# Row-max tiles of a causal attention: diagonal tiles taken out of PSUM by ScalarE and masked by GpSimd, own part buffers, and ScalarE's units unrolled

## The chip, the cores and the metric

One core of a Trainium2 chip runs the whole layer in one launch. The metric is the device time of the execution in microseconds (us), as the median of several runs. Engines are named as in the profile: PE is TensorE (matmuls; PEld its weight loads), DVE is VectorE, ACT is ScalarE, POOL is GpSimd and SP is SyncE, which issues most DMAs.

## What is computed

```python
x = L0_attn_x                                  # 2 x 1024 x 256, f32
q, k, v = x @ Wq, x @ Wk, x @ Wv               # 16 heads, 4 KV heads, head size 16
att = q k^T / 4 + alibi + causal mask          # softmax over keys, y = att v
x = layernorm(x + y @ Wo)
# FFN: shared expert silu(x Wg) * (x Wu) @ Wd, and one of 8 routed experts
x = layernorm(x + shared + routed)
```

The change touches the attention alone, and in it mostly the row maximum that the softmax subtracts.

## The kernel before

**Units.** A batch element with one KV head and its 4 query heads is a unit; there are 8 (`NU`). A query block or a key block has 128 rows, 8 of each. Q and K of a unit lie in SBUF as bf16 parts, so that one matmul with 127 contraction rows gives an accurate score. Three buffers of Q and K (`Q6`, `K6`, `STEP` = 3) take turns.

**Two score passes.** The first pass finds each query row's maximum. `max_tile` (PE) makes the scores with queries on the partitions (L529) in one PSUM bank of 512 columns: up to 512 keys of one head, or several heads side by side where the rows are short. Where the key range reaches the diagonal, a second matmul adds a 128x128 mask of -3e38 above it (L531, identity times `mask_qk`). DVE then reduces the bank to one maximum per row and head (`reduce_tile`, L895). These are 39 tiles a unit, listed by `row_max_tiles`, in 3 banks that PE gets back from DVE in order (`s_amax`). Behind the last tile DVE splits the maxima in three bf16 parts with five small operations that wait for each other (`split_max`, L929 to L939). PE transposes the parts (L520), DVE copies them to `mrow` (L946), and SP sends them by DMA to three rows of Q (`max_rows`, L324). This transpose is the 40th entry of the unit's stream and stands behind the first two tiles (`LEAD`) of the next unit.

The second pass makes the scores again, keys on the partitions, with the maximum already subtracted by those rows (`score`, L543, 36 a unit, 3 banks). ACT takes the exponential into SBUF (L820). POOL sets the upper triangle of a diagonal tile to zero (`mask_probs`, L1156). PE multiplies with V in f32 (`weigh`, L554, below W). ACT copies the two result banks out (L829, L834), and SP stores them.

**Order.** PE runs in one hand-written order. A unit has 9 groups, each a string over S (one second-pass score), M (one row-max entry) and W (the `weigh` of the group before): `SHORT` is `SMSMSMWMS`, `LONG` is `SMSMSMWMSM`. The strings alternate and hold 40 M. The Ms of unit u's groups are the later ones of unit u+1 and then the first 14 of unit u+2 (`AHEAD`), so that row maxima are ahead of their use. Unit 0's 39 and the first 14 of unit 1 run in the prologue. ACT's units 0 to 5 are the body of a hardware loop: two turns of three units (`act.Fori`), with units 6 and 7 behind it as plain code. SP has a loop of the same kind.

**Prologue.** Twelve jobs (`JOBS`) project Q, K and V (L499). Each is split in three bf16 parts by ACT, DVE and POOL (L801, L906, L813 or L914, L1128). The first four go to Q and K of units 0 and 1 directly. Jobs 4 to 11 put their parts in one of three buffers (`parts0`, `NP` = 3), and SP stores them in DRAM (L428), from where later units load them (L305, L311). From the fourth of them on, ACT waits until the buffer's store has landed (`s_pw`). SP issues those stores behind 20 DMAs of the direct path (L376, L384), in program order. Between the jobs PE and DVE do the row maxima of unit 0 in lots (`first_tiles`).

## Time and profile before

| what | value |
|---|---|
| median of 3 runs | 568.68 us (566.39, 571.71, 568.68) |
| profiled execution, its own time | 574.12 us |
| its span, first to last instruction | 572.4 us |
| mean granted TensorE clock | 0.957 |
| DMA packets | 39465, 54.97 MB |

The span is what the trace covers; the 1.7 us beside it lie before the first and behind the last instruction. The profiled execution took 5.4 us more than the median. The attention's units lie between 64 and 290 us of the span, the prologue before and the FFN behind them.

### The profile page before, as it was taken

The numbers are of one execution on the slowest core, as the hardware profiler recorded it, in microseconds if no ns is written. First come the engines' busy times: TensorE is split into PE (matmuls) and PEld (weight loads), VectorE is DVE, ScalarE is ACT, GpSimd is POOL, SyncE is SP. The second block draws the span as 40 slices with busy tenths as digits, with TensorE's granted clock in tenths as the row PEclk, the third lists the DMA queues.
The fourth block names the chain that finished last, engine by engine and source line by source line (L and its number), as shares of the span: only waits on it lengthen the run. The fifth ranks groups of instructions, "written<-read, shape, count | busy, mean of one in ns | idle before, by whom it ended". The sixth has DMA issues, their size and how long they took to land.

```text
span 572.4 us, 7851 instructions
## 1 busy us (share of the span) xinstructions
PE 521.7 (91%) x2538; PEld 259.4 (45%) x2538; DVE 299.7 (52%) x624; ACT 231.4 (40%) x465; POOL 172.3 (30%) x240
## 2 busy tenths in 40 slices
PE   5868899999799999998987899989999999999991
PEld 2433333333233333331245754655666565656661
DVE  1759888888678888882045734212212233333332
ACT  3523376767476767677820121001012222232320
POOL 4413111413031313121201106860003545454543
PEclk9979899999989999999977889998999999999997
DMA  7759501927152727210224600221112222222220
GB/s 219 144 146 313 130 23 49 251 75 207 50 135 78 177 82 181 77 38 21 73 81 149 205 0 1 92 93 38 55 52 60 69 61 74 65 74 65 59 53 27
DMA packets 39465, 54.97 MB, mean 96 GB/s; under 512 B 5887, under 2 KB 27971, under 8 KB 39316
## 3 DMA queue, kind: packets, MB, share of 16 engines
q1 hardware_dynamic: 29792, 30.96, 20.7%
q0 software_dynamic: 5952, 19.56, 11.0%
q10 hardware_dynamic: 3680, 3.94, 2.1%
q8 instruction: 21, 0.34, 0.3%
q14 instruction: 20, 0.16, 0.1%
HBM read 34.76 MB, written 17.52 MB: 91 GB/s over the span
## 4 chain that ended last, share of the span: by engine, by line
PE 80%; DVE 6%; ACT 4%; SPq 3%; issue 2%; DMA 1%; another core or an unknown queue 1%; POOL 1%; POOLq 0%; ACTq 0%; DVEq 0%
PE ps L734 14%; PE ps L554 12%; PE ps L529 11%; PE ps L654 10%; PE ps L543 9%; PE ps L753 7%; PE ps L665 5%; DVE mx L895 4%; PE ps L626 3%; PE ps L499 2%; PE ps L531 2%; PE ps L745 2%; ACT probs L820 2%; PE ps L643 1%; SPq L376 1%
## 5 line engine op out<-in xcount | busy, mean ns | idle before, releaser
L895 DVE TENSOR_REDUCE mx<-ps 128x1 f32<-128x512 f32 (+4 forms) x312 | 184.1, 643 | 39.2 <-PE ps L531 22.8
L820 ACT ACTIVATE probs<-ps 128x512 f32<-128x512 f32 x288 | 153.0, 605 | 74.8 <-PE ps L543 70.1
L529 PE MATMUL ps<-qk_or_dn 127*128 127x512 bf16 (+3 forms) x384 | 119.8, 339 | 4.6 <-DVE mx L895 3.5
L543 PE MATMUL ps<-qk_or_dn 127*128 127x512 bf16 x288 | 101.4, 382 | 6.2 <-ACT probs L820 5.7
L1156 POOL TENSOR_SCALAR_AFFINE_SELECT probs<-probs 128x512 f32<-128x512 f32 x64 | 40.6, 634 | 177.8 <-ACT probs L820 177.8
L734 PE MATMUL ps<-wgu,tmp 128*128 x184 | 82.9, 593 | 0.1
L554 PE MATMUL ps<-probs,Vs 128*32 128x512 f32 x576 | 77.1, 608 | 0.7 <-ACT probs L820 0.7
L529 PEld LDWEIGHTS ps<-qk_or_dn 127*128 127x128 bf16 x384 | 37.8, 99 | 78.7 <-DVE mx L895 65.0
L531 PE MATMUL ps<-cb 128*128 128x128 bf16 x256 | 51.8, 227 | 0.0
L1200 POOL DMA_INDIRECT rows<-acc,tok x23 | 22.5, 979 | 91.5 <-DMA acc<-x_all 46.7
L1084 DVE TENSOR_TENSOR tmp<-tmp,ps 128x512 f32<-128x512 f32 x23 | 15.8, 688 | 65.1 <-PE ps L734 65.1
L734 PEld LDWEIGHTS ps<-wgu,tmp 128*128 128x128 f32 x184 | 33.3, 190 | 33.3 <-issue 33.3
L543 PEld LDWEIGHTS ps<-qk_or_dn 127*128 127x128 bf16 x288 | 27.0, 98 | 43.6 <-ACT probs L820 27.2
L753 PE MATMUL ps<-qk_or_dn,tmp 128*128 x184 | 43.6, 380 | 0.8 <-ACT tmp L876 0.8
L876 ACT ACTIVATE tmp<-ps 128x512 f32<-128x512 f32 x23 | 13.7, 597 | 74.9 <-PE ps L745 74.9
L753 PEld LDWEIGHTS ps<-qk_or_dn,tmp 128*128 128x128 f32 x184 | 34.9, 190 | 15.1 <-issue 11.5
L853 ACT ACTIVATE tmp<-ps 128x512 f32<-128x512 f32 x16 | 9.4, 597 | 66.7 <-PE ps L654 61.0
L531 PEld LDWEIGHTS ps<-cb 128*128 128x128 bf16 x256 | 25.7, 100 | 14.9 <-issue 1.6
L665 PE MATMUL ps<-wsd,tmp 128*128 128x256 f32 x128 | 29.7, 391 | 2.4 <-DVE x_all L1072 2.4
L499 PE MATMUL ps<-probs,yU 128*128 128x512 f32 x48 | 26.3, 686 | 6.1 <-DMA yU<-in_wq 6.1
L654 PE MATMUL ps<-probs,wsg 128*128 128x512 f32 x64 | 31.4, 615 | 0.0
L654 PE MATMUL ps<-probs,wsu 128*128 128x512 f32 x64 | 31.3, 612 | 0.0
(117 smaller groups left out, 467.7 us busy)
## 6 DMA issues: line engine op xcount, KB each, us to landing
wgu<-in_gu POOLq DMA_DIRECT2D x8, 1024.0 KB, 6.4
qk_or_dn<-qparts SPq DMA_DIRECT2D x36, 128.0 KB
yT<-yU SPq DMA_DIRECT2D x16, 256.0 KB, 2.4
qk_or_dn<-in_dn SPq DMA_DIRECT2D x8, 512.0 KB, 8.0
tmp<-xs SPq DMA_DIRECT2D x23, 128.5 KB
qparts<-tmp SPq DMA_DIRECT2D x6, 384.0 KB, 4.3
tmp<-yT SPq DMA_DIRECT2D x34, 64.0 KB
xs<-rows POOLq DMA_DIRECT2D x1, 2056.0 KB, 12.8
```

The lines of the kernel that those rows point to most:

```text
L499: mm = pe.matmul(ps[:, 4 + n % 4, :], w, xTc[:, c, kc, :], start=kc == 0, stop=kc == KC - 1)
L529: mm = pe.matmul(o, q, K6[k][0:KROWS, k0:k0 + w], start=True, stop=not masked)
L531: mm = pe.matmul(o[:, diag:diag + P], id16, mask_qk, start=False, stop=True)
L543: pe.matmul(o, K6[k][0:KROWS, kb * P:(kb + 1) * P], Q6[k][0:KROWS, :, qi * P:(qi + 1) * P], start=True, stop=True).then_inc(s_st, 1)
L554: mm = pe.matmul(ps[32 * j:32 * j + VP, 2 + bank, :], Vs[:, u % STEP, kb, :], probs[:, 4 * (s % 3) + p, :], start=begins, stop=ends, skip_ ...
L654: mm = pe.matmul(ps[:, bank + 2 * (n % 2), :], w[:, kc, f * P:(f + 1) * P], x1T[:, kc, c * CH:(c + 1) * CH], start=kc == 0, stop=kc == KC - 1)
L665: mm = pe.matmul(ps[:, 4 + n % 2, 0:H], hidden_part(c, f)[:, t * P:(t + 1) * P], wsd[:, f, :], start=f == 0, stop=f == FC - 1)
L734: mm = pe.matmul(ps[:, 2 * k + half_i, :], xsT[k][:, kc, :], wgu[:, bass.ds(e * (KC * 2 * I) + (kc * 2 * I + half_i * I), I)], start=kc == ...
L753: mm = pe.matmul(ps[:, 7, 0:H], ehT[j % 2][:, f, :], wdn[:, bass.ds(experts[j] * (FC * H) + f * H, H)], start=f == 0, stop=f == FC - 1)
L820: act.activation(probs[:, 4 * (s % 3) + p, :], ps[:, 4 + (4 * s + p) % SB, :], ACT.Exp, scale=SCALE).then_inc(s_exp, 1)
L895: dve.tensor_reduce(o, ps[:, a_bank(u, t), 0:nh * w].rearrange("p (h w) -> p h w", h=nh), AX.X, ALU.max).then_inc(s_amax, 1)
L1156: pool.affine_select(tile, tile, [[0, HG], [1, P]], ALU.is_ge, zero, base=0, channel_multiplier=-1).then_inc(s_mask, 1)
```

## The change

1. **Diagonal tiles apart.** `row_max_tiles` now lists, for each of the 8 query blocks, one DIAG tile (its 128x128 diagonal block for all 4 heads, one full bank), and the keys left of it as LEFT and RIGHT tiles. This makes 38 tiles, 8 of them DIAG. The mask matmul is gone. ACT copies a DIAG bank to one of two SBUF buffers (`copy_diag`, into `dg`), which frees the bank for PE (`s_dcopy`). POOL writes -3e38 above the diagonal (`cut_diag`). DVE reduces it from SBUF four entries later than its place in PE's order (`reduce_order`, `BEHIND`).
2. **Split spread out.** `split_max` becomes two joins behind the last tile of a unit (`join_max`) and four parts, one ahead of each of the next four tiles. The transpose stands behind six tiles of the next unit (`LEAD` = 6).
3. **Order strings.** 39 M a unit. Nineteen of unit u+2 run in unit u (`AHEAD`), 13 of unit 1 in the prologue, and unit 0 takes `LONG` nine times (45 M).
4. **ACT unrolled.** The copies stand in ACT's order as in PE's, and all eight units are plain code.
5. **Own part buffers.** Jobs 4 to 11 each have a buffer, in the region of `wgu`; ACT's wait for `s_pw` is gone. The direct DMAs of unit 0 now all come ahead of those of unit 1.
6. **POOL.** Its gate and up weight loads and `zero_slots` come one group later.

```diff
-LEAD, AHEAD = 2, 14
+LEAD, AHEAD, FIRST_AHEAD = 6, 19, 13
+BEHIND, ND = 4, 2
+SPLITS = 4
-ORDER = (SHORT, LONG) * 4 + (SHORT,)
+ORDER = (SHORT, LONG) * 4 + ("SMSMSMWS",)
...
+def unit_order(u):
+    return (LONG,) * GROUPS if u == 0 else ORDER
...
 def max_tile(u, k, t):
-                    pe.wait_ge(s_amax, i - 2)
+                    beside, diag = freed(i - 3)
+                    if FREED_BY_ACT[i - 3]:
+                        pe.wait_ge(s_dcopy, diag)
+                    else:
+                        pe.wait_ge(s_amax, beside)
...
-                    if masked:
-                        mm = pe.matmul(o[:, diag:diag + P], id16, mask_qk, start=False, stop=True)
...
+            def copy_diag(u, t, bank):
+                n = NQ * u + A_TILES[t][0]
+                act.wait_ge(s_aps, max_index(u, t) + 1)
+                if n >= ND:
+                    act.wait_ge(s_dmax, n - (ND - 1))
+                act.activation(dg[A_TILES[t][0] % ND], ps[:, bank, :], ACT.Copy).then_inc(s_dcopy, 1)
...
-                    if n >= DIRECT + NP:
-                        act.wait_ge(s_pw[n % NP], 16 * ((n - DIRECT) // NP))
-                    act.activation(parts0[n % NP][0:m, 0, :], ps[0:m, 4 + n % 4, :], ACT.Copy).then_inc(s_ph, 1)
+                    act.activation(parts0[n][0:m, 0, :], ps[0:m, 4 + n % 4, :], ACT.Copy).then_inc(s_ph, 1)
...
-            with act.Fori(0, LOOPS, 1) as it:
-                for k in range(STEP):
-                    step(it * STEP + k)
-            for u in range(LOOPS * STEP, NU):
-                step(u, last=u == NU - 1)
+            for u in range(NU):
+                step(u)
...
 def reduce_tile(u, t):
+                if kind == DIAG:
+                    dve.wait_ge(s_dcut, NQ * u + qi + 1)
+                    dve.tensor_reduce(mxd[:, :, qi], dg[qi % ND].rearrange("p (h w) -> p h w", h=HG), AX.X, ALU.max
+                                      ).then_inc(s_dmax, 1)
+                    return
...
+            def cut_diag(u, t):
+                n = NQ * u + A_TILES[t][0]
+                pool.wait_ge(s_dcopy, n + 1)
+                tile = dg[n % ND].rearrange("p (h w) -> p h w", h=HG)
+                pool.affine_select(tile, tile, [[0, HG], [-1, P]], ALU.is_ge, least, base=0, channel_multiplier=1
+                                   ).then_inc(s_dcut, 1)
```

In the rows below `ps` is PSUM, `qk_or_dn` holds Q and K, and `cb` the constants. PE's order over two groups of unit 0, before:

```order
L529 MATMUL ps<-qk_or_dn 128x512
L543 MATMUL ps<-qk_or_dn 128x512
L529 MATMUL ps<-qk_or_dn 128x384
L531 MATMUL ps<-cb 128x128
L543 MATMUL ps<-qk_or_dn 128x512
L529 MATMUL ps<-qk_or_dn 128x384
L531 MATMUL ps<-cb 128x128
L554 MATMUL ps<-probs,Vs 32x512 x4
```

PE's order in unit 0 after the change (L583 is the row-max matmul, L596 the second-pass score, L607 the `weigh`):

```order
L583 MATMUL ps<-qk_or_dn 128x384
L596 MATMUL ps<-qk_or_dn 128x512
L583 MATMUL ps<-qk_or_dn 128x128 x4
L596 MATMUL ps<-qk_or_dn 128x512
L583 MATMUL ps<-qk_or_dn 128x128 x4
L607 MATMUL ps<-probs,Vs 32x512 x4
```

The mask matmul L531 is gone from the masked tiles, and the diagonal blocks of four heads stand together as four matmuls of 128 columns.

DVE's order from the end of one unit's maxima to the next unit's tiles, before (`mx0`, `mx1` hold maxima, `mparts` the bf16 parts):

```order
L895 TENSOR_REDUCE mx1<-ps 128x1 x4
L929 TENSOR_TENSOR mx0<-mx0,mx1 128x4x4
L932 TENSOR_SCALAR mparts<-mx0 128x32
L934 SCALAR_TENSOR_TENSOR mrest<-mx0,mparts 128x32
L937 CAST mparts<-mrest 128x32
L939 TENSOR_TENSOR mparts<-mrest,mparts 128x32
L895 TENSOR_REDUCE mx0<-ps 128x4
L895 TENSOR_REDUCE mx0<-ps 128x2
L946 COPY mrow<-ps 96x128
```

The same place after the change (`eq` is the region that now holds the diagonal maxima and the joined ones):

```order
L1007 TENSOR_TENSOR mx0<-mx0,mx1 128x4x3
L1010 TENSOR_TENSOR eq<-mx0,eq 128x32
L1016 TENSOR_SCALAR mparts<-eq 128x32
L971 TENSOR_REDUCE mx0<-ps 128x4
L1018 SCALAR_TENSOR_TENSOR mrest<-eq,mparts 128x32
L971 TENSOR_REDUCE mx0<-ps 128x2
L1021 CAST mparts<-mrest 128x32
L971 TENSOR_REDUCE mx0<-ps 128x2
L1023 TENSOR_TENSOR mparts<-mrest,mparts 128x32
L966 TENSOR_REDUCE eq<-dg0 128x4
L971 TENSOR_REDUCE mx0<-ps 128x1
L1030 COPY mrow<-ps 96x128
```

One more small operation, the last four with a reduction between them, and the copy to `mrow` five reductions behind the joins instead of two.

ACT's order in unit 0 after the change, from the middle of the unit (L886 is the exponential, L842 the copy of a diagonal bank, L904 a result bank's copy):

```order
L842 ACTIVATE dg<-ps 128x512
L886 ACTIVATE probs<-ps 128x512 x3
L904 ACTIVATE yU<-ps 128x512
L886 ACTIVATE probs<-ps 128x512
L842 ACTIVATE dg<-ps 128x512
L886 ACTIVATE probs<-ps 128x512 x5
```

Before, this was the body of a loop, with a register instruction between the exponentials and a branch at the end:

```order
L820 ACTIVATE probs<-ps 128x512
L817 REGISTER_ALU
L819 REGISTER_ALU
...
L837 COMPARE_AND_BRANCH
```

Eight copies a unit are added between the exponentials, and register instructions and branch are gone.

## Rows read from the trace of the kernel before

**Rows 1.** The page, part 1: each engine's busy time, share and instructions.
```profile
PE 521.7 (91%) x2538; PEld 259.4 (45%) x2538; DVE 299.7 (52%) x624; ACT 231.4 (40%) x465; POOL 172.3 (30%) x240
```
**Rows 2.** Busy time by stretch, one unit each: length, each engine's busy us, PEclk, DMA, GB/s.
```profile
122.60:151.00 28.40, 27.82 (x191) 10.40 (x190) 23.96 (x45) 19.97 (x38) 6.72 (x11) 1.00 0.49 130
151.00:184.85 33.85, 29.79 (x191) 10.67 (x190) 24.19 (x45) 20.19 (x38) 6.63 (x11) 0.95 0.40 109
241.65:268.80 27.15, 24.89 (x159) 8.04 (x158) 17.64 (x33) 19.81 (x38) 5.08 (x8) 1.00 0.06 21
```
**Rows 3.** Who waited for whom from 122.6 to 151 us: total us, times, longest.
```profile
ACT probs L820 <- PE ps L543: 8.4, 11, 1.3
...
PE ps L520 <- DVE mparts L939: 0.5, 1, 0.5
```
**Rows 4.** Groups by line and shape, same stretch: count, busy us, mean ns, idle before.
```profile
L820 ACT ACTIVATE probs<-ps 128x512 f32<-128x512 f32 x36 | 19.2, 603 | 8.4 <-PE ps L543 8.4
L895 DVE TENSOR_REDUCE mx<-ps 128x1 f32<-128x512 f32 x24 | 15.4, 685 | 1.5 <-PE ps L529 1.1 <-PE ps L531 0.5
...
L531 PE MATMUL ps<-cb 128*128 128x128 bf16 x32 | 6.3, 220 | 0.0
L1156 POOL TENSOR_SCALAR_AFFINE_SELECT probs<-probs 128x512 f32<-128x512 f32 x8 | 5.1, 632 | 21.7 <-ACT probs L820 21.7
...
L895 DVE TENSOR_REDUCE mx<-ps 128x1 f32<-128x384 f32 x8 | 4.1, 551 | 1.5 <-PE ps L531 1.5
```
**Rows 5.** Timeline of PE, 118 to 126 us: start, us, engine, line, what.
```profile
118.08 1.06 PE L554 MATMUL ps<-probs,Vs 128*32 128x512 f32 x8
...
121.37 1.06 PE L554 MATMUL ps<-probs,Vs 128*32 128x512 f32 x8
122.37 0.39 PE L529 MATMUL ps<-qk_or_dn 127*128 127x512 bf16 x1
...
124.20 1.07 PE L554 MATMUL ps<-probs,Vs 128*32 128x512 f32 x8
125.19 0.23 PE L529 MATMUL ps<-qk_or_dn 127*128 127x128 bf16 x1
...
125.67 0.60 PE L543 MATMUL ps<-qk_or_dn 127*128 127x512 bf16 x2
```
**Rows 6.** Timeline of DVE, prologue (54.51) and the end of a unit's maxima.
```profile
54.51 3.07 DVE L895 TENSOR_REDUCE mx<-ps 128x1 f32<-128x512 f32 x5
...
112.56 0.69 DVE L895 TENSOR_REDUCE mx<-ps 128x1 f32<-128x512 f32 x1 [0.47 <-PE ps L531]
113.28 0.18 DVE L929 TENSOR_TENSOR mx<-mx 128x16 f32<-128x16 f32 x1
...
114.26 1.28 DVE L895 TENSOR_REDUCE mx<-ps 128x4 f32<-128x512 f32 x2
```
**Rows 7.** Timeline of ACT, then of PE, 150 to 158 us.
```profile
156.95 1.57 ACT L820 ACTIVATE probs<-ps 128x512 f32<-128x512 f32 x3 [4.47 <-issue]
...
157.60 0.39 PE L543 MATMUL ps<-qk_or_dn 127*128 127x512 bf16 x1 [3.39 <-ACT probs L820]
```
**Rows 8.** Timeline of the prologue: ACT, DVE (two rows), PE.
```profile
35.60 0.59 ACT L801 ACTIVATE tmp<-ps 64x512 bf16<-64x512 f32 x1 [6.12 <-DMA qparts<-tmp]
...
36.22 0.68 DVE L906 TENSOR_TENSOR tmp<-ps,tmp 64x512 f32<-64x512 f32 x1 [3.85 <-ACT tmp L801]
...
59.79 0.21 DVE L946 COPY mrow<-ps 96x128 bf16<-96x128 bf16 x1
...
64.33 0.81 PE L543 MATMUL ps<-qk_or_dn 127*128 127x512 bf16 x3
```
**Rows 9.** Timeline of SP's queue: first and last load of a unit's Q and K.
```profile
124.82 0.30 SPq L299 DMA_DIRECT2D qk_or_dn<-in_zero  x1
...
128.76 2.11 SPq L311 DMA_DIRECT2D qk_or_dn<-kparts  x3
```
**Rows 10.** Timeline of PE in unit 6, where its Ms end.
```profile
261.90 0.23 PE L520 MATMUL ps<-cb,mparts 128*96 128x128 bf16 x1 [1.75 <-DVE mparts L939]
...
265.11 1.06 PE L554 MATMUL ps<-probs,Vs 128*32 128x512 f32 x8
...
267.50 1.06 PE L554 MATMUL ps<-probs,Vs 128*32 128x512 f32 x8
```

240 lines of the change are left out of this document (157 added, 83 removed).

## The prediction

> **What bounds the kernel now.** I read the page first: PE is busy for 91% of the span and DVE for 52% [rows 1]. The page says that a busy PE isn't PE at its peak, so this alone proves nothing; the attention had to be read unit by unit. The table by stretch does that. A unit takes 28.40 us, and PE is busy for 27.82 of them, DVE for 23.96, ACT for 19.97 and POOL for 6.72 [rows 2]. The table of waits of the same stretch shows one wait of PE's matmuls, 0.5 us for the parts of the maxima; ACT waits 8.4 us for PE [rows 3]. The timeline confirms it: between two W (1.0 us each, 121.37 to 122.37) the matmuls stand end to end [rows 5]. So PE is the bound in the units, DVE is next with some 4 us of slack, ACT has 8.
>
> Two places don't fit. The unit from 151 to 184.85 takes 33.85 us, 5.45 more [rows 2]. There ACT stands still for 4.47 us for nothing that the profile shows, and PE waits 3.39 us for it [rows 7]. By the order ACT is then at the branch back to the head of its loop, between units 2 and 3; the clock share of the unit falls to 0.95 [rows 2], which carries the rest. In the prologue ACT waits 6.12 us for a store of parts, and behind it DVE 3.85 us [rows 8].
>
> **1. PE in the units.** The 32 mask matmuls of a unit go. Their mean of 220 ns [rows 4] is latency, since they overlap their neighbours. What one costs is seen where four score and four mask matmuls of 128 columns follow each other: 125.19 to 125.67, 0.48 us for 8, so 0.06 each [rows 5]. That is 32 x 0.06 = 1.9 us. Columns of the real scores stay the same, but the diagonal blocks are cut off: 72 matmuls instead of 48. A 512-column matmul costs (124.20 - 122.37) / 8 = 0.23 at most, with the short gap ahead of W in it, and 0.216 without; four pieces of 0.06 are 0.24. So each cut costs under 0.01 us, 0.2 in all. Net gain 1.7 us a unit.
>
> **2. The wait for the parts.** The chain of five small operations costs DVE 114.26 - 113.28 = 1.0 us [rows 6], and PE's transpose waits 0.5 us for it [rows 3]. In the new order the last part comes right behind the reduction that frees the transpose's bank anyway. PE still waits for one small operation, some 0.25 us. Gain 0.25. The joins read the diagonal maxima, whose last tile has been reduced by then.
>
> **3. Does DVE follow?** Back to back, a reduction of 512 takes (3.07 - 0.69) / 4 = 0.595 us [rows 6]; I take 0.47 for 384, 0.13 less than its 551 against 685 ns [rows 4]. After the change a unit has 30 of the first and 8 of the second: 17.85 + 3.8 = 21.6, and joins, parts and the copy of the row some 1.2: 22.8 us against about 26.5 of PE. Over a LONG group it is tighter: PE needs 9 x 0.216 + 1.1 = 3.05 us, DVE 5 x 0.595 = 2.98. The three banks hold 1.8 us of DVE's work during a W, and a diagonal tile gives its bank back without DVE. So I see small waits in the LONG groups alone, 0 to 0.25 us each, and take 0.1 a unit.
> The reduction from SBUF has no row; the bounds are 0.41 us (half the elements, the nearest small form) and 0.69 (the PSUM duration [rows 4]). I take the PSUM pace, 0.595, since the element count is the same.
>
> **4. Does ACT follow?** The exponentials take 603 ns each, but 36 of them and two copies fill only 19.97 us, so one more costs 0.5 [rows 2, 4]. Eight copies add 4 us: 24 of 26.5. Each stands between two exponentials and delays the next by 0.5. A score needs the exponential three before it. In order of time that has about 0.4 us to spare in the string; the copy behind W in groups 7 and 8 eats it, for up to 0.3 us in SHORT and 0.1 in LONG; I take 0.1 a unit, since a W or DVE may be what PE waits for there anyway. The cut on POOL (632 ns like the select [rows 4]) adds 5 us to 6.7 of 26. Copy and cut together take 1.3 us, while four M entries take PE at least 1.7, so DVE finds the tile ready.
> A rule of the Trainium skill bears on this (SBUF — State Buffer, Who interferes with whom): a VectorE instruction with two SBUF inputs and a GpSimd one that reads SBUF lock each other out, while a reduction doesn't. No row here shows it. By it each of the four small two-input operations could wait out a select of 0.63 us, 1 us a unit at POOL's new share; DVE's slack would take it, and the sum would not move.
>
> **Unit, summed:** 28.40 - 1.7 - 0.25 + 0.1 + 0.1 = 26.65 us. Its range is 26.2 (no new wait, and none for the parts) to 27.5 (each of four LONG groups short by 0.25 us). Units 1 to 5 gain 5 x 1.75 = 8.75 us.
>
> **5. The loop.** Without a branch the 4.47 us and the slow clock behind it go, 5.45 us [rows 2, 7]. The other end of the range is nothing, if straight code stalls as well. Against that: units 6 and 7 and the prologue are straight code already, and 4.47 is ACT's only unexplained wait in the attention.
> The Trainium skill (Advanced Engine Details and Errata, Control Flow Timing) puts a compare-and-branch at about 108 ns. By that the unrolling would be worth 0.1 us instead of 5.45. The same page (ISA Cache) speaks of two cache lines of 256 instructions, which fits a body of some 250; the trace's 4.47 decides.
>
> **6. Unit 0** has 45 Ms instead of 39: six more at 0.2 each, 26.65 + 1.2 = 27.85, a gain of 0.55. **Unit 6** takes 27.15 now [rows 2]. Its Ms end at 21 instead of 27. Groups without M take 265.11 to 267.50 = 2.4 us [rows 10]; with Ms 2.83 (121.37 to 124.20) and 3.05. Four full groups 11.8, the fifth 2.7, the wait for the last transpose 2.0 (1.75 now [rows 10]; there everything is still in a row), four at 2.4 = 9.6: 26.1. Gain 1.1. Unit 7 stays.
>
> **7. Prologue.** The store's wait goes. ACT is then free for job 7 at 29.5 instead of 35.6, PE's transpose of V follows job 8 at 32.7, and DVE waits some 0.5 us instead of 3.85 [rows 8]. But then ACT's queue is longer: its weight loads and the copies of the lots stand ahead of what PE waits for. I give back 1.5 us for these. Of the prologue's 52 reductions 50 remain, 1.2 us less. Against this, the copy to `mrow` now follows five reductions instead of two (1.8 us more), and the first score needs its DMA: 59.79 to 64.33 now hides it behind the 14 Ms [rows 8]; with six Ms behind the transpose it lies open by some 1 us. Sum: 3.4 + 1.2 + 0.6 (jobs at full clock) - 1.8 = 3.4 us. Bounds 0 and 6.
>
> **8. Loads.** The first M of unit u+2 comes after 20 entries instead of 26, that is 13 us after the unit's start instead of 19. The unit starts at 122.6, and its loads are issued from 124.82 to 130.9 [rows 9]; with about 2 us to land they are in by 10.5. POOL's weight load, which shares the DMA engines, moves one group back. Costed at nothing, with 2.5 us of cover.
>
> **Sum:** 8.75 + 5.45 + 0.55 + 1.1 + 3.4 = 19.25. The profiled execution took 574.12; after the change 554.9. The median of the runs shown is 5.4 lower, at 568.68, and 19.25 less is 549.4: I predict 549.5.
>
> **The rivals.**
> A. DVE and ACT bind together. PE's groups shrink to DVE's pace in LONG groups, and the copies push the exponentials. For it: 2.98 against 3.05 us. Against it: the SHORT groups between (4 x 0.595 = 2.4 against 2.83). A unit of 27.5 takes 0.85 off in each of six: 554.6.
> B. Straight code stalls ACT as the loop did, once: 5.45 less, 555. For it: the cause of the 4.47 us isn't in the profile. The change would then not do what it says in that part.
> C. The Q and K loads come late at the new first M. If they land 14 us after the start, each of five units waits 1 us: 554.5.
> D. Slower. The diagonal chain isn't hidden: copy, cut and DVE's wait come in program order on three queues, and POOL's cut stands behind a select that waits for its own exponential. If every diagonal tile holds PE for 0.6 us (one copy), the 56 that run beside units cost 33.6 us, and 549.5 + 33.6 = 583. It turns to a loss from 19.25 / 56 = 0.34 us a tile. Against it: ACT's 8.4 us of waiting a unit hold eight copies of 0.5.
>
> **How the numbers follow.** The forecast has 0.66, A 0.17, B 0.08, C 0.05, D 0.04. Its own range is 544 to 554: the unit at 26.2 or 26.9 and the prologue at 6 or 1. The range of 8 in 10 is 542.5 to 556.5, as A, B and C lie within it. A measurement of this kernel tells about 1% from no change. Faster by over 1% (under 563) are all but D: 0.95. D's mild forms give 0.03 to the same, 0.02 to slower.
>
> **What would show it.** Right: units of 26.65 us with PE busy for nearly all; ACT without a wait of 4 us; no wait of ACT for `qparts`; the first score near 61 us. Wrong in step 3 or 4: PE's row-max matmuls wait for DVE's reduction or ACT's copy for over 1 us a unit, or scores for exponentials. Wrong in step 8: PE's first tile of a unit waits for a DMA. Wrong in step 7: the first score still near 64.

## The result, and the profile after

| what | before | after |
|---|---|---|
| median of 13 runs | 568.53 us (566.01 to 571.71) | 564.92 us (562.08 to 568.06) |
| ratio of after to before | | 0.9941, 95% interval 0.9913 to 0.9969 |
| profiled execution: own time, span | 574.12, 572.4 us | 567.30, 565.6 us |
| first W, last W of the attention | 67.40, 288.85 us | 70.53, 286.44 us |
| last W to the end of the span | 283.5 us | 279.2 us |

The change gained 3.6 us, where 19 were predicted; 564.92 lies outside the range of 542.5 to 556.5. In the two profiles the attention ends 2.4 us earlier. The other 4.4 us lie in the FFN, which the change doesn't touch. Its length varies from 275.7 to 283.5 us over the profiles shown here, so the text below reads the attention by the trace, and takes the ratio for the whole.

The page of the kernel after, parts 1 and 4, and two groups of part 5 (beside [rows 1, 4]):

```profile
PE 511.2 (90%) x2474; PEld 250.9 (44%) x2474; DVE 299.2 (53%) x624; ACT 260.4 (46%) x529; POOL 212.4 (38%) x305
...
PE 71%; DVE 11%; DMA 7%; ACT 4%; issue 3%; SPq 2%; POOL 1%; POOLq 0%; ACTq 0%; DVEq 0%
...
L596 PE MATMUL ps<-qk_or_dn 127*128 127x512 bf16 x288 | 103.6, 392 | 9.0 <-DMA qk_or_dn<-mrow 6.0
...
L966 DVE TENSOR_REDUCE eq<-dg 128x4 f32<-128x512 f32 x64 | 43.3, 677 | 0.0
```

PE is busy 10.5 us less than in [rows 1], as wished, and yet the span is hardly shorter. The third line tells where to look: the scores of the second pass (L596) wait 6.0 us for the DMA from `mrow`, and DMA holds 7% of the chain that ended last. No row of before's units has such a wait.

The table by stretch of after, one stretch for each of units 3, 4 and 5 (beside [rows 2], columns as there; each is as long as its unit and begins a group earlier):

```profile
154.40:182.82 28.42, 26.30 (x183) 9.31 (x182) 23.67 (x46) 23.50 (x48) 11.65 (x20) 1.00 0.50 130
182.82:210.24 27.42, 26.29 (x183) 9.31 (x182) 23.66 (x46) 23.49 (x48) 11.65 (x20) 1.00 0.52 135
210.24:237.33 27.09, 26.29 (x182) 9.31 (x182) 23.68 (x46) 23.49 (x47) 11.65 (x20) 1.00 0.50 136
```

PE is busy for 26.3 us of a unit, where it was 27.8 [rows 2], and DVE and ACT follow with 23.7 and 23.5. But the units take 27.1 to 28.4: 0.8 to 2.1 us of each are waits. From first W to first W, units 0 to 6 take 28.66, 30.91, 26.93, 28.41, 27.43, 27.09 and 27.53 us; before, 28.40, 28.40, 28.38, 33.85, 28.39, 28.40 and 26.68. PE's timeline names the waits (the last bracket is the idle time before the row, and what ended it):

```profile
124.44 0.39 PE L596 MATMUL ps<-qk_or_dn 127*128 127x512 bf16 x1 [2.62 <-DMA qk_or_dn<-mrow]
169.35 0.34 PE L583 MATMUL ps<-qk_or_dn 127*128 127x128 bf16 x3 [0.78 <-DMA qk_or_dn<-kparts]
181.42 0.39 PE L596 MATMUL ps<-qk_or_dn 127*128 127x512 bf16 x1 [1.24 <-DMA qk_or_dn<-mrow]
208.84 0.39 PE L596 MATMUL ps<-qk_or_dn 127*128 127x512 bf16 x1 [0.81 <-DMA qk_or_dn<-mrow]
235.93 0.39 PE L596 MATMUL ps<-qk_or_dn 127*128 127x512 bf16 x1 [0.59 <-DMA qk_or_dn<-mrow]
254.18 0.23 PE L578 MATMUL ps<-cb,mparts 128*96 128x128 bf16 x1 [2.69 <-DVE mparts L1023]
```

In units 1 to 5 the first score waits for the maxima that come through `mrow`, and the last transpose of unit 6 waits 2.69 us for its parts, where it was 1.75 [rows 10]. The view of DMA issues, from 100 to 240 us, says why the maxima are late. Before:

```profile
qk_or_dn<-mrow SPq DMA_DIRECT2D x15, 8.0 KB, 1.9
```

After:

```profile
qk_or_dn<-mrow SPq DMA_DIRECT2D x15, 8.0 KB, 5.0
```

The same 15 transfers of 8 KB land 5.0 us after their issue (median) instead of 1.9. The timeline of POOL's queue and of SP's, after, shows what runs beside them:

```profile
140.46 0.80 POOL L1245 DMA_DIRECT2D wgu<-in_gu  x1
146.74 0.72 POOL L1245 DMA_DIRECT2D wgu<-in_gu  x1
147.27 1.83 SPq L379 DMA_DIRECT2D qk_or_dn<-mrow  x3
```

POOL starts a 1 MB load (5.7 us by the page) 0.5 us ahead of the issue of the three small ones. Before, the loads of this unit started at 130.79 and 137.28, and `mrow` was issued at 144.09, just behind them. In unit 1 it is `zero_slots` that is in the way: its first 2 MB are issued at 109.47 and take 12.2 us by the page, and `mrow`, issued from 116.34 on, lands 6.01 us after the last issue at 118.38. That unit loses more than its wait of 2.62 us, since the granted clock falls behind it (0.94 over the unit): in e7 the same unit has a wait of 2.49 us at full clock and takes 29.14 us. The Trainium skill (DMA: Bandwidth & Descriptors, Queues, rings and completion order) says that every queue runs on the same 16 DMA engines, each of which takes packets from its queues in turn. The trace agrees: from 232 to 234 us the engines are busy for 100% at 396 GB/s, while `mrow` of unit 6 is under way and takes 4.9 us.

The prologue (beside [rows 8]): PE, ACT, DVE twice, and PE's first score.

```profile
32.09 0.61 PE L583 MATMUL ps<-qk_or_dn 127*128 127x512 bf16 x5 [2.27 <-ACT dg L842]
32.54 3.58 PE L553 MATMUL ps<-probs,yU 128*128 128x512 f32 x4
...
38.19 0.63 ACT L874 ACTIVATE wgu<-tmp 64x512 bf16<-64x512 f32 x1 [4.85 <-DVE tmp L982]
...
36.88 0.69 DVE L971 TENSOR_REDUCE mx<-ps 128x1 f32<-128x512 f32 x1 [3.07 <-PE ps L583]
...
62.91 0.21 DVE L1030 COPY mrow<-ps 96x128 bf16<-96x128 bf16 x1
...
66.31 1.03 PE L596 MATMUL ps<-qk_or_dn 127*128 127x512 bf16 x2 [0.44 <-DMA qk_or_dn<-mrow]
```

ACT's 6.12 us for the store [rows 8] are gone, but the first score comes at 66.31 instead of 64.33. There is a ring now. PE's tile waits for ACT's copy of a diagonal tile; PE's job behind it is then late (and at half clock, 3.58 us); DVE waits 3.07 us for the tile behind the job; and ACT's cast waits 4.85 us for DVE's subtraction behind that tile. DVE's waits behind the first reduction add up to 8.8 us, against 7.8 before, though the 3.85 of [rows 8] are gone.

### The profile page after: what moved, and what is told of

It reads as the page before. It is cut to its first block, busy times and chain, and to the rows that moved or that the text cites. A ratio compares the mean times of both kernels' runs of the same rounds, so it can differ in the third digit from the quotient of the medians.

```text
span 565.6 us, 7685 instructions
## 1 busy us (share of the span) xinstructions
PE 511.2 (90%) x2474; PEld 250.9 (44%) x2474; DVE 299.2 (53%) x624; ACT 260.4 (46%) x529; POOL 212.4 (38%) x305
## 4 chain that ended last, share of the span: by engine, by line
PE 71%; DVE 11%; DMA 7%; ACT 4%; issue 3%; SPq 2%; POOL 1%; POOLq 0%; ACTq 0%; DVEq 0%
PE ps L785 14%; PE ps L705 10%; PE ps L607 9%; PE ps L596 7%; PE ps L804 7%; PE ps L583 7%; DVE mx L971 6%; DMA qk_or_dn<-mrow 5%; PE ps L716 5%; PE ps L553 3%; PE ps L677 3%; PE ps L796 2%; ACT probs L886 2%; PE ps L694 1%; DVE eq L966 1%
## 5 line engine op out<-in xcount | busy, mean ns | idle before, releaser
L886 ACT ACTIVATE probs<-ps 128x512 f32<-128x512 f32 x288 | 155.4, 613 | 33.4 <-PE ps L596 33.0
L971 DVE TENSOR_REDUCE mx<-ps 128x1 f32<-128x512 f32 (+3 forms) x240 | 148.2, 649 | 36.2 <-PE ps L583 35.7
L583 PE MATMUL ps<-qk_or_dn 127*128 127x128 bf16 (+3 forms) x576 | 114.4, 284 | 11.9 <-DVE mx L971 6.5
L596 PE MATMUL ps<-qk_or_dn 127*128 127x512 bf16 x288 | 103.6, 392 | 9.0 <-DMA qk_or_dn<-mrow 6.0
L583 PEld LDWEIGHTS ps<-qk_or_dn 127*128 127x128 bf16 x576 | 47.6, 100 | 92.7 <-DVE mx L971 38.4
L607 PE MATMUL ps<-probs,Vs 128*32 128x512 f32 x576 | 78.2, 615 | 0.7 <-ACT probs L886 0.7
L1219 POOL TENSOR_SCALAR_AFFINE_SELECT dg<-dg 128x512 f32<-128x512 f32 x64 | 40.8, 638 | 46.2 <-ACT dg L842 46.1
L596 PEld LDWEIGHTS ps<-qk_or_dn 127*128 127x128 bf16 x288 | 26.6, 98 | 55.1 <-ACT probs L886 33.1
L947 ACT ACTIVATE tmp<-ps 128x512 f32<-128x512 f32 x23 | 13.7, 597 | 74.9 <-PE ps L796 74.9
L842 ACT ACTIVATE dg<-ps 128x512 f32<-128x512 f32 x64 | 39.5, 618 | 14.1 <-PE ps L583 13.9
L966 DVE TENSOR_REDUCE eq<-dg 128x4 f32<-128x512 f32 x64 | 43.3, 677 | 0.0
L553 PE MATMUL ps<-probs,yU 128*128 128x512 f32 x48 | 27.8, 717 | 6.1 <-DMA yU<-in_wq 6.1
## 6 DMA issues: line engine op xcount, KB each, us to landing
xs<-rows POOLq DMA_DIRECT2D x1, 2056.0 KB, 12.2
```

The costliest lines, as they stand in the source:

```text
L553: mm = pe.matmul(ps[:, 4 + n % 4, :], w, xTc[:, c, kc, :], start=kc == 0, stop=kc == KC - 1)
L583: mm = pe.matmul(ps[:, bank, i * w:(i + 1) * w], Q6[k][0:KROWS, h0 + i, qi * P:(qi + 1) * P], K6[k][0:KROWS, k0:k0 + w], start=True, stop= ...
L596: pe.matmul(o, K6[k][0:KROWS, kb * P:(kb + 1) * P], Q6[k][0:KROWS, :, qi * P:(qi + 1) * P], start=True, stop=True).then_inc(s_st, 1)
L607: mm = pe.matmul(ps[32 * j:32 * j + VP, 2 + bank, :], Vs[:, u % STEP, kb, :], probs[:, 4 * (s % 3) + p, :], start=begins, stop=ends, skip_ ...
L886: act.activation(probs[:, 4 * (s % 3) + p, :], ps[:, 4 + (4 * s + p) % SB, :], ACT.Exp, scale=SCALE).then_inc(s_exp, 1)
L966: dve.tensor_reduce(mxd[:, :, qi], dg[qi % ND].rearrange("p (h w) -> p h w", h=HG), AX.X, ALU.max).then_inc(s_dmax, 1)
```

## The experiments

Each ratio is to the kernel before on the same chip, with its 95% interval. The kernel after has 0.9941 [0.9913, 0.9969], but it wasn't run beside any of the experiments: e4, whose trace differs little from after's, has 0.9863. So how much a single edit gives is read from the traces here, and its ratio only says that the sign is right.

### Units: where POOL's loads stand

e1: after, with `zero_slots` and the loads one group earlier, as they were before.

```diff
-                    if s == 4 and u == 1:
+                    if s == 3 and u == 1:
-                    if s in (4, 6) and 2 <= u < NU - 2:
-                        load_gate_up(2 * u - 4 + s // 6)
+                    if s in (3, 5) and 2 <= u < NU - 2:
+                        load_gate_up(2 * u - 4 + s // 5)
```

> The changed kernel with GpSimd's gate and up loads and zero_slots issued one group earlier, where they stood before. Theory 1 (the DMA of the maxima lands late because a 1 MB weight load is on the same DMA engines): the scores' waits for mrow (2.62, 0.26, 1.24, 0.81 and 0.59 us in the changed kernel) vanish or fall under 0.3 us each, unit 1 falls from 30.9 to about 27.5 us, and the time falls by 4 to 6 us, to about 559.5. Theory 2 (it is late because VectorE copies mrow behind five reductions): the waits stay within 0.3 us of what they were and the time stays within 1 us. If the Q and K loads are then what is late, TensorE's first tile of a unit waits for kparts or qparts by over 0.5 us in several units, and the gain is under 2 us.

Measured: 0.9824 [0.9764, 0.9885]. Units 1 to 5 take 26.92, 27.37, 28.03, 27.29 and 26.87 us, 136.5 in all instead of 140.8. The waits for `mrow` behind 124 us are gone (ahead of it two remain, 1.12 and 0.35 us), but in their place the first tile of the next unit waits for its K:

```profile
136.82 0.40 PE L583 MATMUL ps<-qk_or_dn 127*128 127x128 bf16 x4 [1.10 <-DMA qk_or_dn<-kparts]
164.85 0.40 PE L583 MATMUL ps<-qk_or_dn 127*128 127x128 bf16 x4 [1.75 <-DMA qk_or_dn<-kparts]
```

So with 19 entries ahead instead of 14, either place collides with something: group 3 with the loads of Q and K, group 6 with `mrow`.

e6: the second load behind group 8, where neither is under way.

```diff
-                    if s in (4, 6) and 2 <= u < NU - 2:
-                        load_gate_up(2 * u - 4 + s // 6)
+                    if s in (4, 8) and 2 <= u < NU - 2:
+                        load_gate_up(2 * u - 4 + s // 8)
```

(and `zero_slots` at group 3, as in e1).

> The changed kernel with the first gate and up load of a unit at group 4, the second at group 8 (after the copy to mrow), and zero_slots at group 3. Theory 1 (every DMA wait in the units is a 1 MB load beside a small one): waits for mrow and for kparts both stay under 0.3 us in units 2 to 5, a unit takes 26.2 to 26.7 us, and the time is 7 to 9 us under the changed kernel's, 1.5 to 3 under e1_loads_back. Theory 2 (the small DMAs are late by themselves): waits of over 0.5 us remain in each unit.

Measured: 0.9787 [0.9726, 0.9848], the best of the single edits. The table by stretch of e6, units 1 to 5:

```profile
100.82:127.57 26.75, 26.29 (x184) 9.40 (x182) 24.27 (x47) 23.19 (x47) 13.23 (x20) 1.00 0.64 173
127.57:154.06 26.49, 26.24 (x183) 9.28 (x182) 23.72 (x46) 23.28 (x47) 11.75 (x19) 1.00 0.43 117
154.06:181.01 26.95, 26.18 (x184) 9.32 (x182) 23.57 (x46) 23.39 (x47) 11.67 (x19) 1.00 0.51 136
181.01:207.50 26.49, 26.24 (x183) 9.28 (x182) 23.72 (x46) 23.28 (x47) 11.67 (x19) 1.00 0.50 139
207.50:233.99 26.49, 26.24 (x183) 9.27 (x181) 23.72 (x46) 23.28 (x47) 11.67 (x19) 1.00 0.49 139
```

Its DMA issues from 100 to 240 us:

```profile
qk_or_dn<-mrow SPq DMA_DIRECT2D x15, 8.0 KB, 1.8
```

A unit of 26.49 us is the predicted 26.65, with PE busy for all but 0.25. `mrow` lands in 1.8 us again. The same instructions, the same engines: only POOL's second load of each unit and `zero_slots` have moved, and units 1 to 5 take 133.2 us instead of 140.8. With the loads where e6 has them e8 and e10 take 133.6 and 133.5; with after's loads e4, e5 and e7 take 139.1 to 141.3. One wait is left that wasn't expected: in unit 3 the first tile waits 0.67 us for its K (0.92 in e8, 0.68 in e10). Why in this unit alone is open.

### Unit 6: the last transpose

e7: after, with four entries that do nothing ahead of the last transpose, so that groups of scores go first.

```diff
     tiles = max_stream(u + 1)[AHEAD if u else FIRST_AHEAD:] if u + 1 < NU else []
+    if u == NU - 2:
+        tiles = tiles[:-1] + [(NU - 1, None)] * 4 + tiles[-1:]
```

> The changed kernel with the last transpose of the maxima (unit 7's, in unit 6) four entries later in all engines' order, and nothing else. Theory 1 (TensorE's in-order wait of 2.69 us for the parts holds everything behind it): the wait is under 0.3 us, unit 6 takes 25 us instead of 27.5, and the time falls by 2 to 2.7 us. Theory 2 (unit 6 is bound by ScalarE's exponentials from there on): under 0.5 us, as the exponentials take over the wait.

Measured: 0.9868 [0.9801, 0.9935]. Unit 6 takes 23.97 us instead of 27.53, and the wait is 0.29:

```profile
251.74 0.23 PE L580 MATMUL ps<-cb,mparts 128*96 128x128 bf16 x1 [0.29 <-DVE mparts L1027]
```

PE's order is fixed, so a transpose that comes too early holds up scores that were ready. Of the 3.56 us given back, 2.40 are the wait (2.69 less 0.29). The other 1.16 are the clock: after's unit 6 has a granted clock of 0.94, and in e6, with the same order and the same wait of 2.69 at full clock, it takes 26.37.

### The loop and the masks, each by itself

e2: before, with ACT's units as plain code.

```diff
-            with act.Fori(0, LOOPS, 1) as it:
-                for k in range(STEP):
-                    step(it * STEP + k)
-            for u in range(LOOPS * STEP, NU):
+            for u in range(NU):
```

> The kernel before with ScalarE's eight units as plain code and nothing else changed. Theory 1 (the 4.47 us stall belongs to the loop's branch back): no ScalarE wait of over 2 us in the units, and 5.4 us less, about 563. Theory 2 (plain code stalls as well, or the stall is that of one execution): a wait of 3 to 5 us somewhere else, and less than 2 us gained.

Measured: 0.9911 [0.9886, 0.9937]. The unit of 33.85 us now takes 28.85, and no stall is left, here or in any of the 14 profiles without the loop. All three with it (before, e3, e9) have one at the same place: ACT stands 4.47, 2.67 and 4.94 us. So step 5 was right in its cause, and its size is that of one profile. But all units from 0 to 5 take 28.85 instead of 28.40. The timelines of e2, DVE and POOL, at the parts of the maxima (before: [rows 6]):

```profile
114.62 0.18 DVE L934 CAST mparts<-mrest 128x32 bf16<-128x32 f32 x1
114.83 0.65 DVE L936 TENSOR_TENSOR mparts<-mrest,mparts 128x32 bf16<-128x32 f32 x1
...
114.81 0.63 POOL L1153 TENSOR_SCALAR_AFFINE_SELECT probs<-probs 128x512 f32<-128x512 f32 x1 [2.62 <-ACT probs L820]
```

The same subtraction in the kernel before:

```profile
114.15 0.19 DVE L939 TENSOR_TENSOR mparts<-mrest,mparts 128x32 bf16<-128x32 f32 x1
```

The last part takes 0.65 us instead of 0.19, because POOL's select starts 0.02 us ahead of it; before, the select starts at 114.20, just behind. It does so in six of eight units (645 to 651 ns), and PE's transpose waits 0.97 us instead of 0.52. That is the rule of the Trainium skill that step 4 weighed (SBUF — State Buffer, Who interferes with whom): of two such instructions the one that starts first locks the other out. Step 4 said that no row shows it, and that the sum would not move. Here it moves, by 0.45 us a unit. The same section of the Trainium skill counts casts among what can be locked out, and reductions not. The view of one line in e6 agrees (duration in ns: least/median/most):

```profile
L1021 DVE CAST mparts<-mrest x4: 170/449/449, 142.3 to 222.3; 128x32 bf16<-128x32 f32 x4
L966 DVE TENSOR_REDUCE eq<-dg x54: 669/676/680, 70.7 to 245.6; 128x4 f32<-128x512 f32 x54
```

Three of the four casts take 449 ns, each with a select that began 0.22 us ahead; where the select began behind the cast, it takes 170. The 54 reductions from SBUF, with POOL busy for 11.7 us of a unit instead of 6.7, stay within 11 ns. In the new order the parts stand apart, and the transpose doesn't wait for them in units 2 to 5: there DVE's slack does take it.

e9: before, without the mask matmuls (`masked = False`); its row maxima also run over keys behind the diagonal.

> The kernel before with the mask matmuls left out of the row maxima, so that these run over the keys behind the diagonal of a block too, and nothing else changed. It prices the mask matmuls. Theory 1 (TensorE is the bound in the units and a mask costs 0.06 us): a unit takes 26.6 to 26.9 us instead of 28.4, and the time falls by 10 to 12 us. Theory 2 (VectorE's reductions and the 3 banks take over): TensorE's row-max matmuls wait for VectorE by over 0.5 us a unit, a unit takes 27.3 us or more, and the time falls by less than 8 us.

Measured: 0.9893 [0.9831, 0.9956], 5.6 us less where 10 to 12 were expected. A unit takes 27.35 us instead of 28.40, and PE is busy for 26.09 of it, 1.7 less than in [rows 2]. So 32 masks bring 1.05 us here, not 1.9: the transpose's wait for the parts grows from 0.52 to 1.19 us, which gives 0.67 back. With the parts spread out, as in e6, the whole comes through: PE is busy for 26.24 us, 1.58 less than in [rows 2]. So most of the masks' gain comes through only with the parts spread; spreading them alone wasn't run. The units gain 5.9 us up to the first W of unit 7, and 2.9 of them are lost in the prologue (table below): ACT waits 7.79 us for the store instead of 6.12, and two jobs run in part at half clock.

### The prologue: own parts, and the ring

e3: before, with the own part buffers alone (no wait for `s_pw`).

```diff
-                    if n >= DIRECT + NP:
-                        act.wait_ge(s_pw[n % NP], 16 * ((n - DIRECT) // NP))
-                    act.activation(parts0[n % NP][0:m, 0, :], ps[0:m, 4 + n % 4, :], ACT.Copy).then_inc(s_ph, 1)
+                    act.activation(parts0[n][0:m, 0, :], ps[0:m, 4 + n % 4, :], ACT.Copy).then_inc(s_ph, 1)
```

> The kernel before with a part buffer for each of jobs 4 to 11 and nothing else changed. Theory 1 (the prologue's gain is real and the diagonal copies take it back in the changed kernel): ScalarE's wait for qparts is gone, the first second-pass score starts at 59 to 61 us instead of 64.33, and the time falls by 3.5 to 5 us. Theory 2 (VectorE's work bounds the prologue anyway): the first score stays at 63 us or later and the gain is under 1.5 us.

Measured: 0.9882 [0.9861, 0.9903]: this edit alone is better than the whole change. The first W comes at 60.56 instead of 67.40 us, and the last W 9.0 us earlier than before's, where the whole change brought 2.4.

The table has all prologues, from the trace. The first reduction itself varies between 21.1 and 23 us, so the distance from it counts. The fourth column is the time at half clock (a granted clock of 0.5, that is 1.2 of 2.4 GHz) from 20 to 80 us. The last is what that clock costs the projection jobs of the stretch: the four matmuls of a job (L553 in after) take 1.88 to 1.99 us at full clock and up to 3.73 at half, and the excess over 1.94 is added up.

| kernel | first reduction to first score | to first W | half clock | jobs' excess |
|---|---|---|---|---|
| before | 41.8 us | 44.9 us | 13.7 us | 1.0 us |
| e2 (the same prologue) | 41.7 | 44.8 | 13.6 | 1.2 |
| e9, no masks | 46.2 | 49.2 | 17.1 | 2.7 |
| e3, own parts | 35.9 | 39.0 | 3.4 | 0 |
| e12, own parts and unrolled | 36.0 | 39.3 | 3.4 | 0 |
| after; e1, e6, e7 (the same) | 43.3; 41.4, 44.9, 43.5 | 47.6; 45.6, 49.4, 47.1 | 20.5; 13.6, 23.9, 20.5 | 2.1; 0, 3.1, 1.8 |
| e4, late cast | 42.8 | 46.5 | 17.1 | 1.4 |
| e5; e8 (the same), cut first | 41.2; 38.4 | 45.7; 42.7 | 17.1; 13.6 | 1.2; 0 |
| e10, short way of the maxima | 37.8 | 41.1 | 10.2 | 0 |
| e11, unit 0 masked by PE | 38.0 | 42.5 | 13.7 | 0 |
| e13, both | 39.4 | 43.3 | 13.7 | 1.3 |
| e14, e10 with tiles twice | 41.1 | 44.1 | 3.4 | 0 |
| e15, e12 without unit 0's masks | 35.3 | 38.4 | 6.8 | 0 |

Kernels with the same prologue differ by up to 3.5 us, so one profile tells no single microsecond. Most of that is the last column: less the jobs' excess, the four profiles with after's prologue have 41.2 to 41.8 us, and e10, e11 and e13 37.8 to 38.1; only e5 and e8 stay apart, 40.0 and 38.4. What stands out: own parts alone take 6 us off, and the whole change adds 1.5.

e4: after, with ACT's cast of a job behind the diagonal copies of the next lot, so that the copies don't wait for it.

```diff
-                if n >= ACT_CASTS:
-                    act.wait_ge(s_pr, n + 1)
-                    act.activation(parts0[n][0:m, 1, :], rest0[n % 3][0:m, :], ACT.Copy).then_inc(s_pm, 1)
+                if n - 1 >= ACT_CASTS:
+                    late_cast(n - 1)
```

> The changed kernel with ScalarE's cast of job n moved behind the diagonal copies of lot n in the prologue. Theory 1 (in the prologue a diagonal bank comes back late because its copy stands on ScalarE behind a cast that waits for VectorE): TensorE's wait of 2.27 us at 32 us is gone, VectorE's idle time up to 59 us falls by 2 to 4 us, the first score comes at 63 to 64 us instead of 66.3, and the time falls by 2 to 3.5 us. Theory 2 (the prologue is bound by the projections and the DMA issue): less than 1 us.

Measured: 0.9863 [0.9795, 0.9931], and 42.8 us. PE's wait for the copy falls from 2.27 to 1.26 us, but DVE now waits 2.51 and 2.48 us for POOL's cut, since the cut stands behind POOL's subtraction for the cast that comes later. The ring has only moved.

e5: e4, and POOL cuts the diagonal tiles of a lot ahead of its own subtraction.

```diff
+                if n >= FIRST_A:
+                    for t in first_tiles(n):
+                        if is_diag(t):
+                            cut_diag(0, t)
+                pool.wait_ge(s_pm, n + 1)
+                pool.tensor_tensor(lo, rest0[n % 3][0:m, :], md, ALU.subtract).then_inc(s_pl, 1)
```

> As e4_late_cast, and GpSimd masks the diagonal tiles of a lot ahead of its own part of that job instead of behind it. In e4 the wait had moved: VectorE waited 2.5 us twice for GpSimd's cut. Theory 1 (the prologue's loss is the order of the diagonal chain on three queues, copy behind cast on ScalarE and cut behind subtraction on GpSimd): these waits fall under 0.6 us, first reduction to first score takes 39 to 40.5 us (after 43.3, e4 42.8, before 41.8, e3 35.9), and the time lies 2 to 3 us under e4. Theory 2 (the chain isn't what costs there, but VectorE's work and the later copy of the maxima): it stays above 42 us.

Measured: 0.9829 [0.9773, 0.9885], and 41.2 us. DVE's waits are for PE alone, 6.6 us in all; in e8, with the same prologue, 4.0. Between e1 and e8, neither of which has a job at half clock, the distance falls from 41.4 to 38.4 us. By the means of all six profiles, less the jobs' excess, it falls from 41.5 to 39.2. So the ring costs some 2 to 3 us.

### Put together

e8: after with e5, e6 and e7.

> The changed kernel with three of its parts mended at once: POOL's weight loads behind groups 4 and 8 and zero_slots behind group 3 (as in e6), ACT's cast and POOL's cut taken out of the prologue's chain (as in e5), and the last transpose of unit 6 behind four entries that do nothing (as in e7). If the missing microseconds lie in three separate places, as I hold, the gains add: units 1 to 5 of 26.5 to 27.0 us, unit 6 near 23.5, first reduction to first score 41 to 42, and a time of 547 to 551 us (ratio 0.962 to 0.968). The rival is that they share one cause (the granted clock, say, or a wait that moves on): then it comes out near the best single one, 557 us (0.979).

Measured: 0.9687 [0.9646, 0.9728]. The first W comes at 63.91 us, units 0 to 6 take 28.65, 26.87, 26.50, 27.19, 26.59, 26.49 and 24.01, and the last W comes at 269.16 instead of 286.44: 7.1 us of that lie in units 1 to 5, 3.5 in unit 6 and 6.6 ahead of the first W, of which after's two slow jobs are 2.1. The three places are separate and their gains add, as expected; the ratio lies a little above the 0.962 to 0.968 that were.

e10: e8, with the parts of unit 0's maxima in one go, and their transpose behind two entries.

```diff
+def lead(u):
+    return 2 if u == 1 else LEAD
...
-    return own[:LEAD] + [(u - 1, NA - 1)] + own[LEAD:] + ([(u, NA - 1)] if u == NU - 1 else [])
+    return own[:lead(u)] + [(u - 1, NA - 1)] + own[lead(u):] + ([(u, NA - 1)] if u == NU - 1 else [])
```

> e8, and for unit 0's maxima alone the old way: the four parts in one go, and the transpose behind two entries of unit 1 instead of six. If the longer way to mrow sets the first score (mrow was copied at 62.91 instead of 59.79, step 7 of the prediction took 1.8 us for it), the first score comes 1 to 2 us earlier behind the first reduction than in e8 (41 becomes 39.5 to 40), and the time falls by as much, 0.2 to 0.4%. The rival: PE's queue of jobs and tiles sets it, and then the transpose, now without cover, waits for DVE and nothing is gained or up to 1 us lost.

Measured: 0.9615 [0.9571, 0.9659], the first score 37.8 us and the first W 41.1 us behind the first reduction. The W is 1.6 us earlier than in e8, the score 0.6, and 0.9 of the W's is the clock between the two (3.33 us from score to W instead of 4.23). The direction is as expected, and on one chip e10's median is 549.39 us against 553.90, a larger step than the trace shows. But one profile each can't tell a gain of 0.6 us from chance.

e11: e8, with unit 0's diagonal tiles masked by PE and reduced from PSUM.

```diff
-def is_diag(t):
-    return t is not None and t < NA - 1 and A_TILES[t][5] == DIAG
+def is_diag(u, t):
+    return u > 0 and t is not None and t < NA - 1 and A_TILES[t][5] == DIAG
...
+                masked = u == 0 and kind == DIAG
...
+                    if masked:
+                        mm = pe.matmul(ps[:, bank, i * w:(i + 1) * w], id16, mask_qk, start=False, stop=True)
```

> e8, with the diagonal tiles of unit 0 alone done without ACT and POOL: PE adds the mask of -3e38 by a second matmul, as the kernel before does, and DVE reduces the tile out of PSUM in its place. The other seven units keep the new way. If the chain of copy and cut in the prologue is what takes back the gain of the own part buffers (35.9 us from first reduction to first score in e3, 43.3 in the changed kernel), the distance falls from 41 to 36 to 38 us and the time by 3 to 5 us against e8. The rival, that the order of the direct DMAs or the longer way of the maxima does it, expects 40 to 41 and no change of time.

Measured: 0.9669 [0.9628, 0.9711], and 38.0 us: no gain over e8's 38.4, and a median of 553.58 us against 553.90 on the same chip, where 3 to 5 us were expected. Once the ring is untied, taking unit 0's copies and cuts out brings nothing: that they take back the gain of the own parts is refuted.

e13: e10 and e11 in one.

> e10 and e11 in one: the three mended places, the old short way for unit 0's maxima, and unit 0's diagonal tiles masked by PE and reduced from PSUM. If the two do not touch each other, the time is e10's within 0.2% (about 0.961). If the chain of copy and cut was hidden in e11 only because the longer way of the maxima came behind it, the first score comes 1 us or more before e10's 37.8 us from the first reduction, and the time falls to 0.958 or less. In both, the stretch at half clock should tell: 10 us if nothing changes.

Measured: 0.9617 [0.9590, 0.9644], as e10. Its median of 546.86 us is the lowest of all, 21.7 below the kernel before on that chip (568.58).

e12: before, with own parts (e3) and unrolled (e2).

> The kernel before with two parts of the change alone: own part buffers and ACT's units unrolled. Masks, order and loads stay as before. The two single runs gave 5.3 us (e2) and 6.7 us (e3) less. If they are independent: 556 to 558 us (0.977 to 0.981), first W near 60.5, units of 28.4 to 28.9 us and no long unit. That would be 8 us better than the whole change. If the unrolling's gain was already in e3 in part (its stall was shorter), 559 to 561.

Measured: 0.9862 [0.9808, 0.9917], which is less than expected. In the trace the last W comes at 280.03 instead of 288.85 us, 8.8 earlier. The two edits alone brought it 9.0 (e3) and 2.5 (e2) earlier, and e3's 9.0 hold 2.2 us by which its stalled unit was shorter (31.69), which e12 can't gain twice. Of the 5.45 us that the loop's stall costs in before's profile, the lock of e2 takes back 2.7, 0.45 us in each of six units. Whole times are compared on one chip only, for this reason too: from the last W to the end the profiles of e8, e10, e11 and e12, all from one chip, take 279.1 to 282.6 us, and the eleven from the other chip 275.7 to 277.5, with the same FFN.

### The clock: cause or companion

The stretch at half clock was long wherever the prologue was. The kept traces show one thing that it does. In e1 and e7, whose prologue is the same, the last job starts at the same time, in e1 at a granted clock of 1.00 and in e7 of 0.50 (timeline and stretch of e1, then of e7):

```profile
46.16 1.94 PE L553 MATMUL ps<-probs,yU 128*128 128x512 f32 x4
46.00:50.00 4.00, 3.13 (x14) 1.27 (x12) 2.93 (x5) 0.92 (x2) 0.99 (x2) 1.00 1.09 373
...
46.12 3.73 PE L555 MATMUL ps<-probs,yU 128*128 128x512 f32 x4
46.00:50.00 4.00, 4.00 (x10) 1.69 (x8) 1.23 (x2) 0.60 (x1) 0.64 (x1) 0.50 1.08 368
```

The job takes 1.79 us longer, DVE has 1.23 us of work in these 4 us instead of 2.93, and the first score comes some 2 us later. So where a job runs at half clock, the clock is a cause of the late first score. e14 and e15 change the stretch where it covers no job: e14 shortens it, e15 lengthens it. e14: e10, with each row-max tile computed twice, from 37.6 us on (46 in the expectation).

```diff
-                for i in range(nh):
+                for i in list(range(nh)) * (2 if twice else 1):
```

> e10, but PE computes every row-max tile twice, into the same bank, from the lot of job 8 to the last tile ahead of the first score (46 to 62 us). DVE sets the pace there, and a tile done twice takes PE 0.43 us against DVE's 0.6 a tile, so the extra matmuls should fit into PE's waits. If the granted clock is a cause (PE too idle there, clock halves, and the tiles, the transpose and the first scores of unit 0 run at half pace), the time at half clock between 46 and 72 us falls from 10 to some 3 us, the first score comes up to 1 us and the first W up to 2 us earlier behind the first reduction (40.5 in e10), and the time falls by 0.2 to 0.4%. If the clock is only a companion, the extra work changes nothing or costs up to 2 us.

Measured: 0.9669 [0.9635, 0.9703]. The time at half clock falls from 10.2 to 3.4 us, and yet the first score comes at 41.1 instead of 37.8 us: the repeated matmuls hold up the jobs, and DVE waits 6.5 us for PE instead of 4.2. The table by stretch, 46 to 63 us, in e10:

```profile
46.00:63.00 17.00, 11.37 (x54) 4.48 (x56) 15.45 (x38) 6.23 (x12) 6.00 (x10) 0.70 0.71 215
```

And in e14:

```profile
46.00:63.00 17.00, 13.25 (x89) 7.03 (x87) 15.13 (x36) 4.87 (x9) 6.42 (x9) 0.90 0.59 194
```

The granted clock is 0.90 instead of 0.70, and DVE, which sets the pace here, is as busy as it was. In both kernels every job runs at full clock; here the clock's gain, if there is one, is smaller than what the extra matmuls cost (the last job starts 23.8 us behind the first reduction instead of 21.5).

e15: e12, without the masks of unit 0's row maxima.

```diff
-                    masked = diag < w
+                    masked = diag < w and not first
```

> e12 (kernel before, own parts, unrolled), with the mask matmuls of unit 0's row maxima left out in the prologue alone: its maxima then also run over keys behind the diagonal. PE has less to do, by some 2 us. If less work of PE lets the clock fall, the time at half clock between 46 and 72 us grows from 3.4 to 10 us or more, and the first score stays at 36 us from the first reduction or comes later, 36 to 38, in spite of less work, with the time 0 to 0.4% above e12's 0.9862. If the clock follows something else, it stays at 3.4 us, and the first score comes 0 to 1 us earlier, since DVE sets the pace.

Measured: 0.9821 [0.9789, 0.9854]. The time at half clock grows from 3.4 to 6.8 us, and the first score comes 35.3 us behind the first reduction, 0.7 earlier than in e12. No job falls into the longer stretch (49.3 to 56.1 us; the last job begins at 42.5). So a stretch at half clock behind the jobs doesn't make the first score late, as far as one profile each can tell, and one on a job does. It also slows what PE does alone, from the first score to the first W: 4.2 to 4.5 us at half clock in after, e8 and e11, against 3.1 to 3.2 in before, e3, e12 and e14. That is 1.0 to 1.4 us.

## Why the prediction was wrong

By its own steps; W to W where a unit is meant.

| step | predicted gain | in after's trace | lost |
|---|---|---|---|
| 1 to 5, units 1 to 5 (147.4 us before) | 14.2 | 6.6 (140.8) | 7.6 |
| 6, unit 0 | 0.55 | -0.3 (28.66) | 0.8 |
| 6, unit 6 | 1.1 | -0.85 (27.53) | 1.95 |
| 7, prologue to the first W | 3.4 | -3.1 (70.53) | 6.5 |
| sum | 19.25 | 2.4 | 16.85 |

**Step 8 failed, and took 7.6 us**, of which some 1.7 are the clock that fell behind the wait in unit 1. It costed the loads "at nothing, with 2.5 us of cover", and wrote that "POOL's weight load, which shares the DMA engines, moves one group back". It looked only at the loads of Q and K. They were late too: in e1 the first tile waits for K in four units, 0.60 to 1.75 us. It didn't look at the three 8 KB transfers from `mrow`. The change moves them as well, to behind six tiles instead of two, and they sit on PE's path. Their time from issue to landing was 1.9 us in before, where they are issued behind the loads; beside a 1 MB load it is 5.0. e6 moves the load away and has the predicted unit. Rival C had the right kind of cause, with 0.05, but the wrong transfer. Its own test, "PE's first tile of a unit waits for a DMA", came true once, at 169.35 us.

**Step 7 failed by 6.5 us.** Its first term had the right cause and was too small: own parts bring the first score from 41.8 to 35.9 us (e3), of which 1.0 is before's job at half clock, where the step took 3.85 less 0.5, and 0.6 for the clock. The 1.5 us given back for ACT's longer queue and the 1 us for the DMA that lies open stand in its text, but not in its sum 3.4 + 1.2 + 0.6 - 1.8; with them it would give 0.9. They too were sized without the ring. Copy, cast, cut and subtraction stand in a fixed order on three queues, and each waits for another (e4 moved the wait; e4 and POOL's order together freed some 2 to 3 us). This is rival D's mechanism, "copy, cut and DVE's wait come in program order on three queues". It was looked for in the units, where it doesn't occur, and it sat in the prologue. The 0.6 us for jobs at full clock had the wrong sign for after: two of its jobs run in part at half clock. Of the 7.4 us between e3's first score (35.9) and after's (43.3), the traces give 1.9 to the slow jobs (after and e1), 3.0 to the ring (e1 and e8) and 0.6 to the longer way to `mrow` (e8 and e10), for which the step took 1.8. Between e10 and e3 1.9 us are left that no run explains. From the first score to the first W the clock takes another 1.1.

**Step 6 failed for unit 6** in one term and missed another: the wait for the last transpose, taken as 2.0, is 2.69 us, and 1.16 us are the clock, which the step didn't reckon with. Also, the 27.15 us from which it subtracts are a stretch that begins a group earlier; from W to W the unit took 26.68, so the forecast unit of 26.1 was a gain of 0.6 and not of 1.1. The larger point is that the wait could be avoided, for 2.4 us (e7). For unit 0 the LONG strings cost 28.66 instead of 27.85; its row in e10 has PE busy for 27.66 us at full clock, so both PE's work and a wait of 1.0 us (0.79 of it at the transpose) are above the estimate.

**Steps 1 to 5 were right in mechanism, and the unit in size.** It is 26.49 us where nothing collides, against 26.65: PE's work fell by 1.58 us instead of 1.7 and its waits by 0.33 instead of 0.05 net, two small errors that partly cancel. The stall is gone; its 5.45 us were those of one profile, and it costs 3.3 us in e3 and 6.7 in e9. DVE and ACT follow (23.7 and 23.3 us busy of 26.5; DVE was put at 22.8), and the reduction from SBUF takes 677 ns, near the 685 of PSUM. So rivals A and B are out: in e6's units 1 to 5 no row has PE waiting for a copy, a reduction or an exponential for as long as 0.3 us, and no plain code stalls ACT. A gain of the forecast size was there to be had: e8, e10, e11 and e13 gain 3.1 to 3.9%, some 18 to 22 us. But they hold e7's later transpose as well, 2.4 us that the forecast didn't count on. The change as written reached 0.6%.
